# Softmax attention in a macaron block: score products of 64 rows per head, sums in four blocks of 32 rows with the inverse spread by eight transfers, values at the period's end

## The reference

```python
HEADS = 16; DIM_HEAD = 64; scale = DIM_HEAD ** -0.5; EPS = 1e-10
q = split_heads(x @ Wq.T)      # (8, 16, 512, 64); k and v likewise
sim = einsum('bhid,bhjd->bhij', q, k) * scale
m = max(sim, axis=-1, keepdims=True)
e = exp(sim - m)
attn = e / (sum(e, axis=-1, keepdims=True) + EPS)
out = einsum('bhij,bhjd->bhid', attn, v)
return merge_heads(out) @ Wo.T + bo
```

## Time and profile before

| what | us |
|---|---|
| median of three runs | 2223.76 (2223.67 to 2225.62) |
| the profiled execution: its time, its span | 2225.31, 2223.6 |
| PE busy over the span | 1599.6 (72%) |
| DVE busy | 1569.2 (71%) |
| POOL busy, ACT busy | 1028.3 (46%), 912.8 (41%) |
| attention: first score product, last use of `out` | 280.5, 1151.3 |
| reciprocals of attention (64) | 214.6 |

### The profile page before, as it was taken

One profiled execution on the slowest core, in us unless ns is written; L12 is line 12 of the kernel. 1 busy time (PEld: TensorE's weight loads), 2 busy tenths in 40 slices (PEclk: granted clock), 3 DMA queues, 4 the chain that ended last, 5 costly groups with the idle time before them and its releaser, 6 DMA issues. The chain is left out here.

```text
span 2223.6 us, 29789 instructions
## 1 busy us (share of the span) xinstructions
PE 1599.6 (72%) x9139; PEld 934.4 (42%) x9139; DVE 1569.2 (71%) x3212; ACT 912.8 (41%) x2102; POOL 1028.3 (46%) x1332
## 2 busy tenths in 40 slices
PE   0546389999999999999965563158658888830686
PEld 0334134444444444444423343135437767730453
DVE  5887778878788888877878886336467777752563
ACT  0112255555555555555522221035336676610452
POOL 0111245555555555555532224635435555546353
PEclk9889599999999999999987895579879999955898
DMA  6000022222222222222200000122300000001224
GB/s 186 0 0 1 23 63 58 58 58 58 63 59 61 60 59 58 58 58 59 62 9 1 0 0 24 56 77 80 104 16 1 1 1 1 1 32 62 75 81 145
DMA packets 126010, 104.05 MB, mean 47 GB/s; under 512 B 19680, under 2 KB 120480, under 8 KB 125856
## 3 DMA queue, kind: packets, MB, share of 16 engines
q1 hardware_dynamic: 111616, 77.75, 13.6%
q0 software_dynamic: 8704, 18.89, 2.5%
q10 hardware_dynamic: 5536, 5.52, 0.8%
HBM read 29.32 MB, written 22.30 MB: 23 GB/s over the span
## 5 line engine op out<-in xcount | busy, mean ns | idle before, releaser
L770 ACT ACTIVATE at_pT<-at_turned 128x512 f32<-128x512 f32 x512 | 305.6, 597 | 290.3 <-PE at_turned L837 271.2
L669 DVE TENSOR_REDUCE at_nmax<-at_score 128x1 f32<-128x512 f32 x512 | 337.1, 680 | 69.8 <-PE at_score L814 66.8
L648 POOL TENSOR_TENSOR m_rows<-at_pT 128x512 f32<-128x512 f32 x128 | 162.5, 1269 | 375.1 <-ACT at_pT L770 375.1
L691 DVE RECIPROCAL m_rows<-m_rows 128x512 f32<-128x512 f32 x64 | 214.6, 3353 | 37.7 <-ACT m_rows L776 37.7
L875 PE MATMUL at_pv<-at_pT,at_v 128*64 128x512 f32 x1024 | 230.6, 592 | 0.0
L814 PE MATMUL at_score<-at_kh,at_both 128*128 128x512 f16 x512 | 196.7, 385 | 22.6 <-DVE at_nmax L669 17.0
L1056 POOL DMA_INDIRECT by_token<-m_ysb,m_dest x144 | 138.2, 960 | 144.7 <-DVE m_ysb L1136 109.5
L836 PE MATMUL at_turned<-at_both,at_kh 128*128 128x512 f16 x512 | 194.9, 381 | 0.4 <-ACT at_pT L770 0.3
L837 PE MATMUL at_turned<-at_both,at_kl 128*128 128x512 f16 x512 | 194.8, 380 | 0.0
L656 POOL TENSOR_TENSOR m_rows<-m_rows,at_pT 128x512 f32<-128x512 f32 x128 | 162.8, 1272 | 10.6 <-ACT at_pT L770 0.7
L652 POOL TENSOR_TENSOR m_rows<-m_rows,at_pT 128x512 f32<-128x512 f32 x128 | 162.7, 1271 | 10.4 <-ACT at_pT L770 0.5
(11 more groups left out here) (309 smaller groups left out, 3685.0 us busy)
## 6 DMA issues: line engine op xcount, KB each, us to landing
at_both<-at_part_q SPq DMA_DIRECT2D x128, 128.0 KB, 2.4
at_kh<-at_part_k SPq DMA_DIRECT2D x256, 64.0 KB, 2.0
m_xin<-by_expert SPq DMA_DIRECT2D x144, 72.0 KB
at_both<-at_part_q SPq DMA_DIRECT2D x128, 64.0 KB, 2.1
at_kl<-at_part_k SPq DMA_DIRECT2D x128, 64.0 KB
m_rows<-by_token SPq DMA_DIRECT2D x32, 256.0 KB, 4.8
by_token<-m_ysb,m_dest POOLq DMA_INDIRECT x144
m_x<-in_x SPq DMA_DIRECT2D x8, 256.0 KB, 4.7
```

The lines of the kernel that those rows point to most:

```text
L648: nc.gpsimd.tensor_tensor(acc, pT[g % 2][:, head, 0, :], pT[g % 2][:, head, 1, :], ALU.add).then_inc(chain, 1)
L669: nc.vector.tensor_reduce(nmax[head][:, qt:qt + 1], score[use % 2][:], AX.X, ALU.max, negate=True)\
L691: nc.vector.reciprocal(rinv, total).then_inc(rinv_done, 1)
L770: nc.scalar.activation(pT[g % 2][:, head, kt, :], turned[i % 2][:], ACT.Exp).then_inc(exp_done, 1)
```

## The change

Five things change together in `attn_stage`, and nothing outside it.

1. The score products for the maxima read the high parts of q and k alone, straight where `high` wrote them (two buffers each). Each has 64 rows to sum over, head 0 in rows 0 to 63 and head 1 in rows 64 to 127, issued in pairs, each head to its own bank. The low part of q is left out of the maxima, which shifts numerator and denominator alike.
2. All eight columns of maxima lie in one `nmax` of 8 columns. They are turned once a pair, late in the period, and go to `both` in one transfer instead of two.
3. The sums of a pair lie in four blocks of 32 rows by 256 queries (head, half of the queries) instead of two of 64 rows by 512. So `total_out` and the reciprocal (`invert`) go over 256 columns. The inverse, 32 rows by 256 in each block, is copied to the 64 rows of its head by eight transfers of SP (`spread`), each of 32 rows by 256 elements, two for each block. `normalise` waits for them and is moved by one period: it works on g-2 in the period in which it worked on g-1.
4. The values (`values`) are cut into four parts and stand, with the sums ahead of them, behind the last `scores_turned` of the period, around `max_turned` and the projection of v, which now is made in the pair's own period.
5. One `oT`, two buffers of v and fewer semaphores.

```diff
+        total, packed, rinv = mem["w_attn"][:, 2, 0:HALF], mem["w_attn"][:, 2, HALF:SEQ], mem["w_attn"][:, 2, SEQ:2 * SEQ]
...
+                def spread(g):
+                    sp.wait_ge(packed_done, g + 1)
+                    if g:
+                        sp.wait_ge(o_done, g)
+                    for head in range(2):
+                        for half in range(2):
+                            first = (2 * head + half) * QUAD
+                            for to in (head * DH, head * DH + QUAD):
+                                sp.dma_start(rinv[to:to + QUAD, half * HALF:(half + 1) * HALF], packed[first:first + QUAD, :])\
+                                  .then_inc(rinv_in, 16)
...
+                def invert(g):
+                    dve.wait_ge(total_done, g + 1)
+                    if g:
+                        dve.wait_ge(rinv_in, 16 * R_DMAS * g)
+                    nc.vector.reciprocal(packed, total).then_inc(packed_done, 1)
+
+                def normalise(g):
+                    dve.wait_ge(pv_done, g + 1)
+                    dve.wait_ge(rinv_in, 16 * R_DMAS * (g + 1))
+                    if g:
+                        dve.wait_ge(out_done, g)
+                    nc.vector.tensor_tensor(oT[:], pv[:], rinv, ALU.mult).then_inc(o_done, 1)
...
+                def scores(g, qt):
+                    if qt == 0:
+                        pe.wait_ge(hi_done, 2 * g + 2)
+                    if g or qt:
+                        pe.wait_ge(s_read, 8 * g + 2 * qt)
+                    for head in range(2):
+                        rows = halves[head]
+                        nc.tensor.matmul(score[head][:], head_of[0][g % 2][rows, qt * P:(qt + 1) * P], head_of[1][g % 2][rows, :],
+                                         start=True, stop=True).then_inc(s_done, 1)
...
                 for g in PERIODS:
                     for i in range(UPP):
-                        if live(g + 1):
-                            scores(g + 1, i)
                         if live(g):
                             scores_turned(g, i)
-                        if i == 1 and live(g):
-                            max_turned(g, 1)
-                        if i == 2 and live(g + 2):
+                        if i % 2 == 0 and live(g + 1):
+                            scores(g + 1, i // 2)
+                        if i == 1 and live(g + 2):
                             project(g + 2, 0)
-                        if i == 3:
-                            if live(g - 2):
-                                output(g - 2)
...
+                        if i == 3 and live(g - 2):
+                            output(g - 2)
+                        if i == 5 and live(g + 2):
+                            project(g + 2, 1)
+                    if live(g - 1):
+                        add_up(g - 1)
+                        values(g - 1, 0)
+                    if live(g + 1):
+                        max_turned(g + 1)
+                    if live(g - 1):
+                        values(g - 1, 1)
+                    if live(g):
+                        project(g, 2)
+                    if live(g - 1):
+                        values(g - 1, 2)
+                        values(g - 1, 3)
```

More of the change, by code:

```diff
@@ L597, in _, with q_rows @@
                 clear_spent(sp, mem)
-                def to_rows(g, which, part_i):
-                    src = part[which]
+                def q_rows(g):
                     k = g % RING
+                    sp.wait_ge(hi_done, 2 * g + 1)
                     for head in range(2):
[L603 to L612, removed]
@@ new lines, in q_rows, with k_rows @@
+                    sp.wait_ge(lo_done, 2 * g + 1)
+                    for head in range(2):
+                        sp.dma_start(both[k][DH:P, 0, head, :], rest_of[0][halves[head], :]).then_inc(q_in[k], 16)
+                def k_rows(g):
+                    k = g % RING
+                    sp.wait_ge(hi_done, 2 * g + 2)
+                    for head in range(2):
+                        for half in halves:
+                            sp.dma_start(kh[k][half, head, :], head_of[1][g % 2][halves[head], :]).then_inc(k_in[k], 16)
+                    sp.wait_ge(lo_done, 2 * g + 2)
+                    for head in range(2):
+                        sp.dma_start(kl[k][0:DH, head, :], rest_of[1][halves[head], :]).then_inc(k_in[k], 16)
@@ L781, in _ @@
                         exp(g, 1)
-                        exp(g, 2)
                     if live(g + 2):
@@ L791, in _ @@
                     if live(g):
[L792 to L797 removed]
+                        values_in(g)
             @block.tensor
@@ L866, in values @@
                         pe.wait_ge(total_done, g)
+                    pe.wait_ge(m_out, min(g + 2, PAIRS_ALL))
                     for head in range(2):
-                        last = nc.tensor.matmul(sums[halves[head], :], ones[:], psum[g % 2][:, head, :], start=True, stop=True)
+                        for half in range(2):
+                            first = (2 * head + half) * QUAD
+                            last = nc.tensor.matmul(sums[first:first + QUAD, 0:HALF], ones[:],
+                                                    psum[g % 2][:, head, half * HALF:(half + 1) * HALF], start=True, stop=True)
                     last.then_inc(sums_done, 1)
-                    pe.wait_ge(v_out, g + 1)
-                    if g:
-                        pe.wait_ge(o_done, g)
-                    for kt in range(TPB):
-                        for head in range(2):
-                            last = nc.tensor.matmul(pv[halves[head], :], vv[g % 4][:, kt, halves[head]], pT[g % 2][:, head, kt, :],
-                                                    start=(kt == 0), stop=(kt == TPB - 1))
-                    last.then_inc(pv_done, 1)
+                def values(g, kt):
+                    if kt == 0:
+                        pe.wait_ge(v_out, g + 1)
+                        if g:
+                            pe.wait_ge(o_done, g)
+                    for head in range(2):
+                        last = nc.tensor.matmul(pv[halves[head], :], vv[g % 2][:, kt, halves[head]], pT[g % 2][:, head, kt, :],
+                                                start=(kt == 0), stop=(kt == TPB - 1))
+                    if kt == TPB - 1:
+                        last.then_inc(pv_done, 1)
                 def output(g):
```

228 lines of the change are left out of this document (94 added, 134 removed).

## The result

The change takes 2469.34 us (median of 4 runs, 2464.07 to 2475.8) against 2224.69 for the kernel before beside it: 1.1094 times as long (95% interval 1.106 to 1.1128), 245 us more. The direction was forecast, the size was not: it lies above the range's 2425. The profiled execution took 2475.8 us, 6.5 more than the median.

A forecast was written before the change was run, and what follows sets the result against it. PE's work bounds the kernel before; after the change a DVE and SP loop does. 15.1 + 0.65 (clock) - 13.45 = 2.3 us a period, times 62, plus 4, gives about 2370 us; range 2288 to 2425.

The forecast's parts named there:

- The circle: In attention, normalisation, reductions, reciprocal, eight SP transfers and the next normalisation form a loop of 15.1 us a period.
- PE has turned the maxima by then: In the loop, PE's turning is ready about 6.4 us after normalisation starts, so DVE does not wait for it.
- PE standing at the output: PE waits about 3 us each period at the output projection for DVE's normalisation.
- 11.8: PE's own work in us per attention period after the change, shape changes included.
- The sums: PE's sums of 0.91 us, at half the columns and four blocks side by side, save 0.45, else nothing.
- PE's saving: PE alone would need 1.65 us less per attention period than now.
- the pairs: Eight score products become four pairs running side by side on PE, saving 0.87 us a period; if not, nothing.
- the changes of shape: Some nine more moves between array shapes on PE cost 0 to 0.6 us a period, taken as 0.2.
- The 11.4 us for DVE's work: DVE's reductions, maxima, low parts, reciprocal and normalisation in one period before the change, summed from their durations.
- The clock: PE's clock falls behind the gap in most periods, slowing the output and third pair: 0.65 us a period, bounds 0 to 1.8.
- that the clock holds: Rival: same loop in attention without a clock fall, 2330 us (2285 to 2345), chance 0.27.
- That the transfers cost little: Rival: the eight SP issues are cheap, at 0.2 us each about 2142 us; chances 0.09 faster, 0.08 slower up to 2285.

The follow-up runs named there:

- e3: The change plus 36 unread products of 128 columns on PE per period, ahead of the output projection: 2323.24 us, 1.079 times the kernel before.
- e2: The change with four of the eight transfers of the inverse left out, half its rows unwritten: 2144.52 us, 0.9965 times the kernel before.
- e1: The change with sums in two blocks again and without the eight transfers of the inverse: 2135.15 us, 0.9934 times the kernel before.
- e4: The change with normalisation moved behind the third pair of reductions and output projection to the period's last tile: 2154.48 us, 1.0012 times the kernel before.
- e10: The change with four of the eight transfers issued by ScalarE instead of SP: 2158.95 us, 1.0043 times the kernel before.
- e6: e1 with score products of all 128 rows, the other head's half of q being zeros: 2214.06 us, 0.9945 times the kernel before.

## Why the prediction was right in direction and wrong in size

**The circle: right, and a little short.** Shorten it or move its wait and the loss goes: undisturbed periods are 13.19 without transfers, 12.87 with four, 13.05 with two queues and 13.37 with the wait moved. Issues of 0.63 and the landing of 1.9 came as taken. The circle at full clock measures 15.4 instead of 15.1 (e3, and the shortest full periods of the change itself). The missing 0.3 is at "PE has turned the maxima by then": DVE waits 0.44 us for that turning.

**PE standing at the output: right, somewhat too large.** 2.6 us of wait a period for about 3 forecast, because PE's own work is 12.9 us (e2's undisturbed periods) and not 11.8. The sums did save what was forecast, nearly: 0.57 us for them (1011.07 to 1011.64) instead of 0.91.

**PE's saving: mis-sized, without weight here.** "I take 0.87" for the pairs and "0.2" for the changes of shape were wrong. Row pairs do run side by side; the changes of shape cost 0.1 us each and eat it. The Trainium skill's rule (TensorEngine Tiling (Array Packing), Key Properties: a change of tiling mode drains the engine) was the better guide, and I set it aside on the ground of rows that show only changes in the array's columns. In the change 15.4 us of circle hide it. In e1, where the circle is gone, it decides: -0.7% and not the some -3.5% that 12.25 us of work (the 11.8, and the 0.45 of the sums, which e1 leaves out) would give. The 11.4 us for DVE's work is too high as well: it adds durations of instructions that overlap (its busy share of 80.67 is 10.9 us a period), which weighs nothing here either.

**The clock: the step that failed.** "Bounds are 0 and 1.8 us a period; I take 0.65." It measures 1.45 on the mean of the full periods, and e3, which takes nearly all of it away, confirms the sign and the order of size. The path is the one named, the third pair behind the slow output: 1.38 us in the period shown (4.10 against 2.72). But the clock fell in 52 of 60 periods, at a price of 1.3 to 1.9 us in 44 of them and of 2.6 to 2.8, beyond the upper bound, in 8. The mechanism was right and its size was not.

**Long issues: missing.** A further 0.46 us a period is from single issues and landings that take longer, by up to 1.4 us. The earlier trace rows showed one undisturbed period, from which all issues were taken, and the sum has no term for the others. In the kernel before they occur as well (an issue of 64 KB of k took up to 1.49 us where 0.60 is usual), and its period doesn't show them.

The sum, by measured terms: 15.4 (circle) + 1.45 (clock) + 0.46 (long issues) = 17.3, less 13.51 (before, where one period in eight takes 13.96), is 3.79 us in each of the 60 full periods, 227 us. The last three periods are 13.5 longer together, attention's two ends 6.2 and the rest of the kernel 3.6; that gives the 250.5 between the two profiled spans; between the medians it is 245. The forecast had 2.3 times 62, and 4. With the clock at its forecast 0.65 the time would have been about 2421, within the range; without the long issues alone, about 2442, still above it.

The rivals: that the clock holds was refuted (0.91). That the transfers cost little was refuted by 5.03 us for eight. The Trainium skill's rule on transfers to separate partition halves (DMA: Bandwidth & Descriptors, Rules for kernel authors) had no share that the trace shows: they landed 1.9 us after issue, as those of 64 KB did (2.0).

## What to carry to other kernels

Where the result of a transfer is consumed in the same turn of a software pipeline, write down the whole circle, issues on the one queue included, and compare it with the bound engine's work; here moving the consumer (e4) or splitting the queue (e10) took back nearly all of the loss with every transfer kept. Put the scatter of single issues, not one clean period, into any term on the critical path. And if TensorE will stand in each period, price the slow products behind the gap near the upper bound, since they lie on the same circle.

## What the runs showed of the hardware that was not expected

- A change between products of 128 and of 64 rows costs 0.1 us each way (0.31 and 0.32 against 0.22 us from start to start), so two 64-row products side by side save next to nothing over two of full height when they alternate with others (e1 against e6).
- Behind a wait of 2.18 us the clock was at its lower level: output projection 1.87 us instead of 0.89, products of 512 columns 0.43 from start to start instead of 0.22, until 1008.60 in the period shown. The length of the wait alone doesn't tell: in the period from 729.19, PE waited 2.54 us ahead of the output and the clock stayed at 1.00; in the next it waited 2.25 and the period's clock was 0.90. What decides between them the runs don't show. With the gap filled by unread products the clock was 1.00 in 58 of 60 periods.
- An issue of SP is 0.63 us for 32 KB, 0.60 for 64 KB and 0.71 for the row of maxima, and two queues issue side by side (2.64 and 2.44 us for four each, started 0.1 us apart). Single issues take up to 1.4 us longer; issues or landings are late in 42 of 60 periods of e3 and in 33 of the change. The cause stays open.
